# Sixteen matmuls of ones at the start, an earlier tap, three later y_low, and a split wait in the last output tile

## The reference

```python
x = x + blocksparse_linear(layernorm(x))     # 512x512 weight, 32x32 blocks off where mask sum is 0, plus bias
x = x + ffn(layernorm(x))                    # gate/up 512->1792, silu(gate)*up, down 1792->512; int weights, (w-z)*s
x = x + mamba2(layernorm(x))                 # in_proj to gate, x, B, C, dt; causal conv of 4 taps, silu
                                             # 128 heads of 64, state 128, 8 groups, chunks of 128 tokens
                                             # y = diag part + part of the carried states + D*x
                                             # y = y*rsqrt(mean(y^2)+eps)*norm_w*silu(gate); y @ out_proj.T
x = x + ffn(layernorm(x))                    # the same weights again
```

## Time and profile before

| what | us |
|---|---|
| median of three runs | 2114.71 |
| the three runs | 2114.70, 2115.32, 2114.71 |
| the profiled execution | 2115.85 |
| span of the profiled execution, first to last instruction | 2114.1 |
| TensorE busy in it | 2067.3 |
| VectorE, ScalarE, GpSimd busy | 1656.5, 1424.1, 887.6 |
| mean granted TensorE clock (1 = full) | 0.998 |

### The profile page before, as it was taken

The page is one execution under the profiler, slowest core; times in us unless marked ns, Lnnn a source line. Parts: engine busy times, 40 slices in busy tenths (PEclk is TensorE's granted clock), DMA queues, the critical chain, the costliest instruction groups (busy, mean ns, idle before and its releaser), DMA issues.

```text
span 2114.1 us, 35693 instructions
## 1 busy us (share of the span) xinstructions
PE 2067.3 (98%) x12366; PEld 1703.4 (81%) x12366; DVE 1656.5 (78%) x2676; ACT 1424.1 (67%) x2690; POOL 887.6 (42%) x616
## 2 busy tenths in 40 slices
PE   7999998999999999999999999999999999989999
PEld 6788876788888888888888888888888888878887
DVE  7655557888888888888888888888888888876554
ACT  4322268878787878778787877877877878742221
POOL 1221214445454545454454544454545555422121
PEclk9999999999999999999999999999999999999999
DMA  5543225445444444444444444445444444455341
GB/s 204 176 139 136 78 85 184 151 140 158 147 138 154 139 154 148 150 160 133 142 156 150 144 155 134 150 154 162 139 155 140 154 149 145 148 172 172 131 147 40
DMA packets 160095, 307.06 MB, mean 145 GB/s; under 512 B 14528, under 2 KB 47552, under 8 KB 159680
## 3 DMA queue, kind: packets, MB, share of 16 engines
q1 hardware_dynamic: 159936, 305.00, 44.4%
HBM read 299.70 MB, written 5.24 MB: 144 GB/s over the span
## 4 chain that ended last, share of the span: by engine, by line
PE 78%; DVE 10%; issue 5%; ACT 4%; POOL 1%; DMA 1%; DVEq 0%; ACTq 0%; SPq 0%; POOLq 0%
PE ring L1016 30%; PE ring L1104 14%; PE bank L410 6%; PE bank_e L410 6%; PE yt L1085 5%; PE st L1069 4%; PE bank_e L422 3%; PE yt L1091 3%; PE bank L422 3%; PE xt L1056 3%; DVE xc L1458 1%; DVE ce L1511 1%; DVE em L1519 1%; DVE ygs L1538 1%; DVE bc L1458 1%
## 5 line engine op out<-in xcount | busy, mean ns | idle before, releaser
L1016 PE MATMUL ring<-m_lnt,w_sb 128*128 128x512 f32 x3456 | 858.9, 398 | 5.5 <-ACT sz L1265 2.5
L1016 PEld LDWEIGHTS ring<-m_lnt,w_sb 128*128 128x128 f32 x3456 | 630.1, 188 | 134.0 <-issue 3.1
L1688 POOL TENSOR_TENSOR w_sb<-w_raw,w_sb 128x512 fp32r<-128x512 f32 x288 | 428.4, 1490 | 162.3 <-ACT w_sb L1243 162.0
L1705 POOL TENSOR_TENSOR ysq<-ysq,y 128x512 f32<-128x512 f32 x126 | 169.8, 1348 | 637.2 <-ACT y L1299 637.2
L1104 PE MATMUL ring<-wo,ygs 128*128 128x512 f32 x1536 | 372.2, 392 | 5.6 <-DVE ygs L1538 3.3
L1104 PEld LDWEIGHTS ring<-wo,ygs 128*128 128x128 f32 x1536 | 289.2, 189 | 68.0 <-issue 7.8
L1458 DVE SCALAR_TENSOR_TENSOR xc<-ring,cw,xc 128x511 f32<-128x511 f32 (+2 forms) x384 | 286.8, 747 | 52.3 <-ACT xc L1255 43.2
L1285 ACT ACTIVATE cum_b<-cum_b,cum_q 128x128 f32<-128x128 f32 x1024 | 312.5, 390 | 0.0
L1243 ACT ACTIVATE w_sb<-w_raw 128x512 fp32r<-128x512 f32 x288 | 178.2, 620 | 48.0 <-DMA w_raw<-w_in 47.8
L1693 POOL TENSOR_TENSOR wo<-wo_raw,wo 128x512 fp32r<-128x512 f32 x128 | 191.1, 1493 | 1.6 <-ACT wo L1311 1.6
L1085 PE MATMUL yt<-em,x_dt 128*64 128x128 f32 x2048 | 183.9, 279 | 3.6 <-DVE state L1499 3.5
(11 more groups left out here) (198 smaller groups left out, 2891.9 us busy)
## 6 DMA issues: line engine op xcount, KB each, us to landing
w_raw<-w_in SPq DMA_DIRECT2D x288, 256.0 KB, 3.4
cum_b<-c_t SPq DMA_DIRECT2D x128, 512.0 KB, 4.6
ce<-e_t SPq DMA_DIRECT2D x128, 384.0 KB, 4.5
wo_raw<-w_out SPq DMA_DIRECT2D x128, 256.0 KB, 3.0
f_gu_q<-gu_w SPq DMA_DIRECT2D x28, 512.0 KB, 3.5
f_gu_zr<-gu_z SPq DMA_DIRECT2D x28, 512.0 KB, 4.3
f_gu_sr<-gu_s SPq DMA_DIRECT2D x28, 512.0 KB, 5.3
f_dn_q<-dn_w SPq DMA_DIRECT2D x28, 256.0 KB, 3.4
```

What stands on the lines that cost most here:

```text
L1016: mm = nc.tensor.matmul(dst[:], w_sb[:, u % WR, wp, k * P:(k + 1) * P], lnt[:, xp, k, b * S:(b + 1) * S], start=(i == 0), stop=(i == 3 * K ...
L1688: nc.gpsimd.tensor_tensor(w_sb[:, u % WR, 1], w_raw[:, u % NR], w_sb[:, u % WR, 0].bitcast(F32), ALU.subtract).then_inc(w_lo, 1)
```

## The change

TensorE's program begins with a wait for the four memsets and sixteen 128x128x128 matmuls of ones by ones into bank 2, without reading the result. The last-but-three output tile (31, 0) waits at first for three of its four pairs, and for the fourth before its tenth matmul. ScalarE's `tap(("b", 1))` moves in step 3 from behind `w_high` of the C tile to ahead of `activate_x(4)`. VectorE's `y_low(0)`, `y_low(1)` and `y_low(2)` move in steps 2, 3 and 4 from the head of the step to behind `carry(k)`.

```diff
@@ Mixing.tensor
             def tensor(self, pe, n):
+                pe.wait_ge(consts_zero, 4)
+                for _ in range(16):
+                    nc.tensor.matmul(bank[2][:, 0:P], ones[:], ones[:], start=True, stop=True)
                 pe.wait_ge(consts_ready, 6)
                 pe.wait_ge(self.rowsum_done, 1)
@@ Mixer.tensor, project_out
-                    pe.wait_ge(yg_lo, HALF * (i + 1))
-                    pe.wait_ge(wo_lo, HALF * (i + 1))
+                    early = 1 if (i, t) == (K // HALF - 1, 0) else 0
+                    pe.wait_ge(yg_lo, HALF * (i + 1) - early)
+                    pe.wait_ge(wo_lo, HALF * (i + 1) - early)
                     for m, (j, (yp, wp)) in enumerate((j, ab) for j in range(HALF * i, HALF * (i + 1))
                                                       for ab in PASSES):
+                        if early and m == 3 * (HALF - 1):
+                            pe.wait_ge(yg_lo, K)
+                            pe.wait_ge(wo_lo, K)
                         mm = nc.tensor.matmul(dst[:], ygs[:, j % OR, yp, t * P:(t + 1) * P], wo[:, j % WOR, wp],
@@ Mixer.scalar, step k
                     if k + 1 < K:
                         if k % 2:
                             exponent(k + 1)
+                        if k == 3:
+                            tap(("b", 1))
                         activate_x(k + 1)
                         activate_z(k + 1)
...
                     for unit in bc_units(k):
-                        tap(unit)
+                        if k != 3:
+                            tap(unit)
@@ Mixer.vector, step k
-                    if 2 <= k <= K + 1:
+                    if HALF < k <= K + 1:
                         y_low(k - 2)
...
                         carry(k)
                     if k == 0:
                         conv(("x", 2))
+                    if 2 <= k <= HALF:
+                        y_low(k - 2)
```

## The result

| | before | changed |
|---|---|---|
| median of 20 runs, us | 2114.93 | 2118.36 |
| lowest, highest | 2112.54, 2117.79 | 2116.75, 2120.55 |
| profiled execution, us | 2115.85 | 2118.35 |
| span, us | 2114.1 | 2116.6 |
| mean granted clock | 0.998 | 0.995 |

The ratio is 1.0015 (95% interval 1.0009 to 1.0020): 3.4 us slower. The forecast was 2112.0, in a range of 2108.9 to 2113.8. Both the size and the sign were missed.

The account below looks back on a forecast made before the run. TensorE, busy 98% of the span, was taken as the bound, so time returns only where it idles or runs at half clock. Tap 2.2, ones 0.5, split 0 and y_low nothing sum to 2.7 us: 2112.0, range 2108.9 to 2113.8.

Parts of the forecast that it names:

- The ones: First stage: sixteen matmuls cost nothing, raise the clock early, masks up to 0.95 us earlier; 0.5 us won, ends 0 and 2.3.
- The tap: Long stage, step 3: earlier B tap lets conv start 3.4 us earlier, first output tile 2.2 us earlier; ends 1.5 and 2.9.
- The y_low: Long stage, steps 2 to 4: moving them is worth nothing beside the early tap; 0.9 us for step 4's without it.
- The split: Tile (31, 0): nine matmuls fill the wait, 2.1 us won, a clock fall loses 2.1; taken as 0, ends +2.1 and -1.3.
- The price of the fall: Behind tile (31, 0): clock down 6.8 us, 4.2 us of dense work under it, 2.1 us lost.
- The rivals: Four: clock holds behind split tile, 0.31; ones hold it to first tile, 0.17; slower, 0.03; ones do nothing, 0.12.
- The one on the slower side: Before the last tiles: clock stays down twice 6.8 us or falls again, costing 6.8 us; 2116.7 us, chance 0.03.
- the upper end of the range: 2113.8 us: the forecast with 0 for the ones, 1.5 for the tap and 0.5 lost behind the split tile.

Follow-up runs that it names:

- the single run: Only the sixteen matmuls of ones added to the kernel before: median 2113.74 us against 2114.94, ratio 0.9985 to 1.0003.
- Where ScalarE's part was removed: Kernel before plus ones in five places, early tap, ScalarE normalising tiles 2 and 3 before rounding gate/up weights: 2109.52 us against 2115.09; with split wait, 2109.82.
- the parts that help: Kernel before plus sixteen ones, eight and six between transposes, early tap, twelve ones before first output tile, fourteen before (31, 0): 2110.05 us against 2114.92.

## Why the prediction was wrong

*The ones: right in kind, the term somewhat too small.* They ended at 7.9 and cost nothing, the tile started 1.2 us earlier (0.95 foretold), the clock was down again by then and back before 21 us. I had 0.5; the trace shows 1.3, the single run 1.2. I had the clock come back at the same moment as before; when it comes back varies from trace to trace. The second tile starts at 21.60 to 22.34 in the four traces with the sixteen ones and no more, on average 22.1, and at 22.30 to 23.54 in the seven without, on average 23.0. So 0.9 us is the better size, and the 1.3 has luck in it.

The Trainium skill ("TensorE: Matmul & The Clock Gate", Part 4: PE-mode transpose) says that transposes do not count for the clock as matmuls do. By that rule the clock would be down at the first tile, and the trace of the changed kernel agrees: it fell at the second group of transposes. That the transposes are the reason is not shown, since TensorE also stood idle for 2.07 us between the two groups, and in the trace of the split alone the clock fell at a pause of 2.50 us that had matmuls ahead of it (326 us). The first eight transposes themselves ran at 2.4 GHz. With ones between the groups the clock was up at the first tile (2.96 us).

*The tap: right in kind, 1.6 in place of 2.2, and the second step that failed.* I pushed the reload of the z weights by 0.67; it was 1.5, since GpSimd also took 0.7 longer. And the longer pause of TensorE ahead of the output tile was not in the sum at all. I had written that the whole chain up to that tile moves. The tile does, but what stands before it on TensorE moves more: in the changed kernel `states(4)` came 1.25 us earlier and the tile 0.29 later, and the difference is a pause in which the clock can fall. It fell there in the changed kernel, over the whole tile, and filling the pause gave 2.4 us back. I had taken from the earlier trace rows that waits of 2.47 us bring no fall. That was one trace: in others it fell behind waits of 2.1 to 2.5 us.

*The y_low: the step that failed first.* It said "Put at nothing". I listed what moves up when `y_low` leaves the head of the step, and for what TensorE waits, but not ScalarE: `activate_z` of tile k+1 waits for `y_low(k-2)`, as the third buffer of `sz` is free only then. Moved behind `carry(k)`, `y_low(0)` comes 8 us later, at 347.24 instead of 339.20, and ScalarE idles 4.5 us. Where only the three are moved, `y_low(2)` holds up tile 5 in the same way, and they cost 5.0 us. In the company of the other parts `y_low(0)` alone stalls ScalarE, and they cost 3.3. These 3.3 us and the 2.4 of the clock make up most of the 6.4 between forecast and result.

*The split: near 0, in part by luck.* The mechanism is the one given: a fall of the clock behind the row sums, ScalarE's normalised tiles late next. The row of the last three tiles came 1.6 us earlier in the stage and took 1.5 longer. But 28.0 us equals 28.1 only because the profile before has the long fall; against the 26.7 to 26.9 of the other traces the split loses. Where ScalarE's part was removed, VectorE took its place, which the prediction had not listed. The price of the fall was taken from the one in the profile of before, which the other traces show to be the longest kind.

*The rivals.* The one on the slower side had the right means, a fall of the clock more, and the wrong place: the last tiles, where it was the first output tile. None of the rivals had a new wait of ScalarE, though each moved instruction should have had its waiters listed. Two readings were off without consequence: the windows of the earlier trace rows place the fall from 1861.84 to 1868.66, which leaves its length of 6.8 us, and the upper end of the range comes to 2113.7 by its own terms.

## What to carry to other kernels

When an instruction is moved later, search for every wait on the semaphore that it raises, those of buffers to be freed among them, and not only for the consumer of its result. On a TensorE that is busy 98% of the time, look at how long each pause becomes: shifting work earlier ahead of a fixed wait makes the pause longer, and a pause of 3 to 4 us cost 1.6 to 2.5 us more in the clock. A few matmuls of ones into the bank that the next tile overwrites filled such pauses at next to no cost here (the first tile came 0.1 to 0.4 us later than with the sixteen alone). By subtraction they gave more than the reordering: 4.9 us for the parts that help, of which the tap alone had 1.1.

## What the runs showed of the hardware that was not expected

The granted clock fell in or behind pauses of TensorE, most of them of 2.1 to 4.2 us, and not by their length alone. The pause of 2.3 to 2.4 us at 285 us brought a fall in nine of fourteen profiled executions; one of 2.1 us at 326 did in one trace, two of 1.0 and 0.8 us close together at 331 did in another, and the tap's of 2.9 ahead of the first output tile did not. The clock came back after different times, for the most part after 3.4 or 6.8 us: tile (31, 0) took 4.18, 4.38, 4.43, 4.55, 4.57 and 5.46 us in traces that differ in nothing there. The same pause of 3.9 us ahead of the first output tile gave 4.57 us in one kernel and 5.46 in two others. A price read from one profiled execution is one draw of several. Twelve float32 matmuls of ones, 128x128x128, held the clock over a pause: they take 2.8 us at 2.4 GHz (24 records in 2.84), 0.24 each.

It stays open why the split alone has a median 1.2 us above before. The interval holds 0. The lower mean clock of its runs (0.9973 against 0.9984) speaks for more time at 1.2 GHz, and its trace has falls at 285 and 326 us that the one before has not; whether the split has to do with them is not shown.
